# Row maxima moved from the seam into the projection's batches

## The reference

```python
q = jnp.einsum('oc,bct->bot', Wq, target) + bq[None, :, None]   # target = layernorm(x)
k = jnp.einsum('oc,bcs->bos', Wk, source) + bk[None, :, None]   # source = ctx_2048
v = jnp.einsum('oc,bcs->bos', Wv, source) + bv[None, :, None]
dot = jnp.einsum('bhdt,bhds->bhts', q, k) / math.sqrt(HEAD_DIM)
mask = target_mask[:, :, :, None] * source_mask[:, :, None, :]
dot = mask * dot - (1.0 - mask) * NEG                           # NEG = 1e6
amap = jax.nn.softmax(dot, axis=-1) * mask
out = jnp.einsum('bhts,bhds->bhdt', amap, v)
```

## Time and profile before

| | us |
|---|---|
| median of 3 runs | 1266.68 (1265.74 to 1266.74) |
| profiled execution | 1268.15 |
| its span | 1266.3 |
| PE, DVE busy in the span | 1089.0, 1033.0 |
| ACT, POOL busy in the span | 672.6, 515.0 |
| first score matmul | 170.10 |

### The profile page before, as it was taken

How to read it: one execution, slowest core, us unless ns; L and a number is a source line. 1 busy time by engine, 2 the same in 40 slices (tenths; PEclk the granted TensorE clock), 3 DMA queues, 4 the chain that set the end, 5 groups by cost and what they waited for, 6 DMA issues and landing times. The chain is left out here.

```text
span 1266.3 us, 14046 instructions
## 1 busy us (share of the span) xinstructions
PE 1089.0 (86%) x4802; PEld 424.1 (33%) x4802; DVE 1033.0 (82%) x1568; ACT 672.6 (53%) x787; POOL 515.0 (41%) x403
## 2 busy tenths in 40 slices
PE   4977689999999999778999976999999997189586
PEld 2543112222222222134444433444444443134232
DVE  5679779999999999378999964887888888776898
ACT  1655148888888888946566652110000000786896
POOL 2765221535435436520101014878888883000021
PEclk9989569999999999999999996999999999599889
DMA  9799852446446444132111101121211110000011
GB/s 325 246 306 334 258 181 93 131 129 200 119 141 195 129 146 121 49 122 109 34 51 49 35 20 46 56 64 53 67 54 62 61 55 17 1 1 1 9 59 66
DMA packets 74215, 132.89 MB, mean 105 GB/s; under 512 B 18848, under 2 KB 37664, under 8 KB 73632
## 3 DMA queue, kind: packets, MB, share of 16 engines
q1 hardware_dynamic: 74144, 132.00, 32.4%
HBM read 107.58 MB, written 22.02 MB: 102 GB/s over the span
## 5 line engine op out<-in xcount | busy, mean ns | idle before, releaser
L821 DVE TENSOR_REDUCE mneg<-ps_m 128x1 f32<-128x512 f32 x512 | 324.9, 683 | 38.2 <-PE ps_m L738 34.2
L1383 PE MATMUL ps_y<-kv,toeplitz_sb 128*128 128x512 f32 x640 | 280.4, 597 | 9.8 <-POOL kv L1295 9.8
L696 ACT ACTIVATE probs<-ps_s 128x1024 f32<-128x1024 f32 x256 | 250.7, 1023 | 39.7 <-PE ps_s L760 39.6
L1383 PEld LDWEIGHTS ps_y<-kv,toeplitz_sb 128*128 128x128 f32 x640 | 121.4, 192 | 156.7 <-issue 156.7
L760 PE MATMUL ps_s<-qk_stack 128*128 128x512 bf16 x512 | 138.9, 386 | 23.2 <-ACT probs L696 17.5
L738 PE MATMUL ps_m<-qk_stack 64*128 64x512 bf16 x512 | 126.0, 411 | 14.5 <-DMA qk_stack<-mask_k 12.5
L770 PE MATMUL ps_o<-probs,v_all 128*17 128x512 f32 x1024 | 135.6, 602 | 0.2 <-ACT probs L696 0.2
L1295 POOL TENSOR_TENSOR kv<-vT,ctxT_sb 128x2048 f32<-128x2048 f32 x32 | 118.7, 3710 | 41.2 <-PE ps_y L1383 33.4
L1001 PE MATMUL ps_g<-w,xT_f 128*128 128x512 bf16 x512 | 119.3, 382 | 11.4 <-DVE h_f L1167 7.9
L1449 DVE TENSOR_TENSOR z<-ps_y,ctxT_sb 128x1024 f32<-128x1024 f32 x64 | 77.9, 1217 | 48.1 <-PE ps_y L1383 48.1
L1348 ACT ACTIVATE w_anchor<-w_f 128x512 f32<-128x512 f32 x32 | 20.1, 628 | 180.6 <-DMA w_f<-in_w 180.6
(11 more groups left out here) (159 smaller groups left out, 1624.7 us busy)
## 6 DMA issues: line engine op xcount, KB each, us to landing
qk_stack<-qk_parts SPq DMA_DIRECT2D x192, 128.0 KB, 4.0
w_sweep<-in_w SPq DMA_DIRECT2D x8, 1536.0 KB, 10.9
qk_parts<-qk_part SPq DMA_DIRECT2D x48, 256.0 KB, 4.6
w_sweep<-in_w SPq DMA_DIRECT2D x16, 768.0 KB, 5.2
w_sweep<-in_w SPq DMA_DIRECT2D x16, 512.0 KB, 3.7
toeplitz_sb<-in_toeplitz SPq DMA_DIRECT2D x32, 256.0 KB, 2.6
w_f<-in_w SPq DMA_DIRECT2D x32, 256.0 KB, 2.9
v_rows<-vp SPq DMA_DIRECT2D x8, 544.0 KB, 10.3
```

The source lines that it names most:

```text
L696: nc.scalar.activation(pr[:, k % 2, 2 * slot:2 * slot + 2, :], S[:, 2 * slot:2 * slot + 2, :], ACT.Exp).then_inc(exp_done, 1)
L821: nc.vector.tensor_reduce(mneg[:, h, tc, hd:hd + 1], M[:, bank(j), :], AX.X, ALU.max, negate=True).then_inc(max_red, 1)
L1383: mm = nc.tensor.matmul(Y[:, q % 3, l2, :], T[:, g % 2, (lt - m) * P:(lt - m + 1) * P], kv[:, g % 2, m, :], start=(m == 0), stop=(m == lt))
```

## The change

1. **Maxima.** 38 of the 48 tiles of the seam are taken inside batches 3 to 7, in pairs (`ahead`), four pairs a batch at fixed places: behind the keys, behind the queries, in the middle of the values and behind them. Batch 7 has three. A pair uses banks 0 and 1 of `ps_m` and waits until the pair before is reduced. Unit 0 is then finished in batch 6, its maxima are turned in batch 7 and its row copied by ACT there. Ten tiles of unit 1 are left for `vector_first`, now behind the weight totals. `ps_a` of the projection takes all eight banks of PSUM, and `ps_m` lies over its banks 4 to 6; the values, which used banks 4 to 7, now share banks 6 and 7 (`VP`), so that the pairs have banks 4 and 5.
2. **Engines.** ACT normalises the rows (scale and a shift `xa_shift`) and masks the values. In batch 7 its three weight sums stand ahead of the first copy.
3. **Loads.** Unit (0,0) is loaded in batch 1, (0,1) in batch 3, (1,0) in batch 7 between the stores of keys and of queries, and (1,1) at the end. The mask rows and leading parts of a unit have one semaphore (`qk_lead`), the rest another (`qk_rest`). A store of parts is one DMA of 768 KB instead of three of 256 KB.
4. **Memory.** `qk_r` is gone, the rest is written over `qk_f`; the buffers are ordered so that those freed first lie under stack 2 and attention's own first loads.

```diff
 def load_unit(core, sp, b, h):
     slot = 2 * (b % 2) + h
+    sp.wait_ge(core.qk_stored[b % 2], 32 * (b // 2 + 1))
+    for a in range(2):
+        for dst, src in ((core.Q, core.mask_q), (core.K, core.mask_k)):
+            heads = dst[slot][:, QUAD * a:QUAD * (a + 1), :]
+            sp.dma_start(heads[SIDE * a + LEAD:SIDE * (a + 1):STEP],
+                         src[:, b].unsqueeze(1).to_broadcast([HD, QUAD, L])).then_inc(core.qk_lead[slot], 16)
...
-                         .rearrange("d s x l -> d s (x l)"), both[:, a]).then_inc(core.qk_loaded[slot], 16)
+                         .rearrange("d s x l -> d s (x l)"), both[:, a])\
+                .then_inc((core.qk_lead if blk < LEAD else core.qk_rest)[slot], 16)
...
         for b in range(B):
+            if b == B - 1:
+                load_first(sp)
             store_parts(b, KS)
             if b + RING < B:
                 load_ctx(b + RING)
+            if b == B - 1:
+                load_next(sp, 0)
             store_parts(b, QS)
...
-            if b == B - 3:
                 sp.wait_ge(rows_stored, 32)
-                sp.wait_ge(qk_stored[0], 96)
                 load_unit(core, sp, 0, 0)
-            if b == B - 1:
+            if b == 3:
                 load_unit(core, sp, 0, 1)
...
         for b in range(B):
+            if b == B - 1:
+                for m in range(3):
+                    sum_weights(b, m)
             part1(b, KS)
-            if b:
+            if 1 <= b < B - 1:
+                normalise(b + 1)
                 sum_weights(b, 0)
+            if b == B - 1:
+                rows_of_first_max(act)
             part2(b, KS)
             part1(b, QS)
-            if b:
+            if 1 <= b < B - 1:
                 sum_weights(b, 1)
             part2(b, QS)
+            mask_values(b)
...
         for b in range(B):
             keys(b)
+            ahead(pe, b, 0)
             if b == 0:
                 values(b)
             queries(b)
+            ahead(pe, b, 1)
             if b:
                 values(b)
+            ahead(pe, b, 3)
...
+    def ahead_pairs(b, part):
+        n = 4 * (b - FIRST) + part - (b == B - 1)
+        return range(max(n, 0), n + 1) if b >= FIRST and not (b == B - 1 and part == 0) else range(0)
+
+    def tensor_pair(pe, q):
+        v, h = q // (TILES // 2), q // (TILES // 2)
+        if q % (TILES // 2) == 0:
+            pe.wait_ge(qk_lead[h], LEADS)
+        if q == TILES // 2:
+            pe.wait_ge(mrow_ready, 1)
+        if q:
+            pe.wait_ge(max_red, 2 * q)
+        for a in range(2):
+            leading_products(pe, h, (2 * q + a) % TILES, a)
...
+def load_first(sp):
+    load_batch(sp, 0, 0)
+    place_max(sp, 0, 0, 0)
+def load_next(sp, h):
+    if h == 0:
+        sp.wait_ge(wsum_ready, 3 * B)
+        load_unit(core, sp, 1, 0)
+    else:
+        sp.wait_ge(k_done, B)
+        sp.wait_ge(v_done, B)
+        load_weights(sp, 0, 0)
+        sp.wait_ge(f_ready, 2 * B)
+        load_unit(core, sp, 1, 1)
+        load_weights(sp, 1, 1)
```

More of the change, by code:

```diff
@@ L197, in store_parts @@
             sp.wait_ge(p3_ready, nth(b, s))
-            for j in range(3):
-                sp.dma_start(core.parts[s, b, j].rearrange("(ct p) l -> p ct l", p=P), part[:, b % 2, s, j])\
-                    .then_inc(qk_stored[b % 2], 16)
+            sp.dma_start(core.parts[s, b].rearrange("j (ct p) l -> p (j ct) l", p=P),
+                         part[:, b % 2, s].rearrange("p j ct l -> p (j ct) l")).then_inc(qk_stored[b % 2], 16)
         def store_values(b):
@@ new lines, in place_max @@
+    def place_max(sp, v, slot, h):
+        sp.wait_ge(mrow_ready, v + 1)
+        for a in range(2):
+            row = SIDE * (1 - a) + MAX_ROW
+            sp.dma_start(Q[slot][row:row + STEP + 1:STEP, QUAD * a:QUAD * (a + 1), :], mrow[UH * a:UH * (a + 1)])\
+                .then_inc(m_placed[h], 16)
+    def load_first(sp):
[12 more added lines that the diff above has]
+            load_weights(sp, 1, 1)
@@ L663, in gpsimd, with rows_of_first_max @@
             batch(b, b % 2, b == 0, b == B - 1)
+    def rows_of_first_max(act):
+        act.wait_ge(m_turned, 1)
+        nc.scalar.activation(mrow[:], RT0[0:2 * UH, 0:L], ACT.Copy).then_inc(mrow_ready, 1)
     def scalar(act):
@@ L667, in rows_of_max @@
             act.wait_ge(m_turned, v + 1)
-            if not same(v, 0):
-                act.wait_ge(m_placed[1 - h], 32 * before)
+            act.wait_ge(m_placed[1 - h], 32 * before)
             nc.scalar.activation(mrow[:], RT[0:2 * UH, 0:L], ACT.Copy).then_inc(mrow_ready, 1)
-        rows_of_max(0, 0, 0)
-        act.wait_ge(rows_stored, 32)
         act.wait_ge(q_done, B)
         act.wait_ge(v_done, B)
-        act.wait_ge(p3_ready, 2 * B)
+        for p in range(2):
+            act.wait_ge(v_stored[p], 16 * (B // 2))
         def evacuate(u, h, G, bu):
@@ L716, in scalar, with tensor_ahead, leading_products @@
         over_batches(act, batch)
+    def ahead_pairs(b, part):
[9 more added lines that the diff above has]
+            pe.wait_ge(max_red, 2 * q)
+        for a in range(2):
+            leading_products(pe, h, (2 * q + a) % TILES, a)
+    def tensor_ahead(pe, b, part):
+        for q in ahead_pairs(b, part):
+            tensor_pair(pe, q)
+        if b == B - 1 and part == 0:
+            pe.wait_ge(m_split, 1)
+            for tc in range(LT):
+                mm = nc.tensor.transpose(RT0[0:2 * UH, tc * P:(tc + 1) * P], mm16[:, 0, tc, :], core.ident16[:])
+            mm.then_inc(m_turned, 1)
     def tensor_first(pe):
-        pe.wait_ge(qk_loaded[0], LOADS)
+        for q in range(AHEAD, 3 * TILES // 4):
+            tensor_pair(pe, q)
         pe.wait_ge(vt_ready, LT * B)
-        for tile in range(HALF):
-            max_tile(pe, 0, 0, tile, HALF + tile)
-        for tile in range(HALF, TILES):
-            max_tile(pe, 0, 0, tile, tile - HALF)
+        pe.wait_ge(o_cleared, 1)
+    def leading_products(pe, slot, tile, bank_):
+        a, hd, tc = place(tile)
+        rows = slice(SIDE * a, SIDE * (a + 1))
+        nc.tensor.matmul(M[:, bank_, :], Q[slot][rows, hd, tc * P:(tc + 1) * P], K[slot][rows, hd, :],
+                         start=True, stop=True).then_inc(max_mm, 1)
     def max_tile(pe, v, slot, tile, j):
-        a, hd, tc = place(tile)
         n = TILES * v + tile
@@ L732, in max_tile @@
             pe.wait_ge(mrow_ready, v)
-        elif TURN_SLOT <= j < TURN_SLOT + 2:
+        elif TURN_SLOT <= j < TURN_SLOT + 2 or (v == 1 and j < 2):
             pe.wait_ge(max_red, n - 1)
-        elif not (same(v, 0) and tile < 3):
+        else:
             pe.wait_ge(max_red, n - 2)
-        rows = slice(SIDE * a, SIDE * (a + 1))
-        nc.tensor.matmul(M[:, bank(j), :], Q[slot][rows, hd, tc * P:(tc + 1) * P], K[slot][rows, hd, :],
-                         start=True, stop=True).then_inc(max_mm, 1)
+        leading_products(pe, slot, tile, bank(j))
     def tensor(pe):
@@ L856, in vector @@
     def vector(dve):
-        for tile in range(HALF):
-            reduce_tile(dve, 1, 1, tile, HALF + tile)
         def batch(b, par, first, last):
```

259 lines of the change are left out of this document (132 added, 127 removed).

## The result

| | before | after |
|---|---|---|
| median, 11 runs each on one chip, us | 1266.43 (1264.89 to 1267.32) | 1269.11 (1267.96 to 1272.01) |
| ratio to before | | 1.0023 [1.0015, 1.0032] |
| profiled execution, span | 1268.15, 1266.3 | 1270.36, 1268.6 |
| T, weights of batch 7 used | 125.4 | 144.4 (forecast 141.3) |
| first exponential | 172.53 | 175.98 (forecast 171.5) |

The change makes the kernel 2.7 us slower. The forecast was 1265.6, so it is 3.5 us off. Of the 3.45 us by which the first exponential is late, 2.9 are still there at the end of attention.

The account below looks back on a forecast made before the run. The projection was taken as bound by DMA through the masks batches wait for, and the first exponential as deciding the end. T +16.0 (9.5 + 5.2 + 1.3) and a tail 17.0 shorter gave -1.0: 1265.6 us, range 1257 to 1273.

Parts of the forecast that it names:

- The step that failed: how much of two unit loads is new ahead of T: Projection: the early loads of units (0,0) and (0,1) put 3.2 MB more ahead of T, 9.5 us later at 334 GB/s.
- A path called hidden: Batch 3: PE waits for unit 0's leading parts until 80.7 us, queries and values behind; hidden, since mask 4 lands at 92.
- 5.2: From 71.3 to 84 us SP issues only unit (0,0) into an empty queue; 1.7 MB are missing, 5.2 us.
- 1.3: Batches 0 and 1: ACT's longer chain with POOL costs 3 us, fewer store issues return 1.7; net +1.3, bounds 0 and +4.
- The tail: From T to the first exponential: 47.2 us before, T+30.2 after, so 17.0 us shorter.
- Chain (b): PE's chain from T: pairs of maxima and batch 7's values, first score at T+28.9, exponential at T+31.3 or T+29.6.
- a mixture: PE's clock in batch 7, between half and full: full for the second half of values gives T+29.6, half gives T+31.3.
- (a): SP's chain from T: stores and unit (1,0), values issued at T+24.4, landed T+28.8, first exponential T+30.2; taken to decide.
- B: Rival: the engines catch up the queue time lost from 71 to 84 us; T only 9.5 later, 1259 us; chance 0.27.
- C: Rival: the loop of mask, queries, POOL, store and later mask sets the pace, batches 5 to 7 4.8 later; 1270.5; chance 0.10.
- D: Rival: unit loads cost their issue time even in a full queue, 7.6 us more than the forecast, 1273 us; chance 0.08.
- A: The forecast itself: the queue takes back what the seam gives; 1265.6 us, own range 1262 to 1269.5; chance 0.55.

Follow-up runs that it names:

- e2: Changed kernel with unit (0,1) loaded in batch 5 instead of batch 3, behind the weights of batch 7; 1264.97 us, ratio 0.9980.
- e11: Kernel before with the load of unit (0,0) also made a second time, in batch 3; ratio 1.0067.
- e12: Changed kernel with a unit's 12 transfers of parts issued ahead of the wait for the mask tables and of its mask rows; ratio 1.0010.
- e10: Changed kernel with unit (0,0) loaded in batch 2 instead of 1, mask tables still stored in batch 1; 1274.74 us, ratio 1.0065.
- e3: Changed kernel with the projection's 38 reductions reading 8 of 512 columns, so their maxima are not the true ones; 1271.28 us, ratio 1.0033.
- e9: Kernel before with the two mask tables stored in batch 0 instead of batch 1; ratio 0.9995.
- e6: Changed kernel with tables stored in batch 0, unit (0,1) loaded in batch 5, and batch 7's values and weights ahead of unit (1,0); 1257.3 us, ratio 0.9928.
- e1: Changed kernel with batch 7's queries' parts and values stored, then unit 0's weights loaded, ahead of unit (1,0); 1266.19 us, ratio 0.9995.
- e5: Kernel before with the engine edit alone: ScalarE normalises the rows and masks the values; ratio 1.0017.
- e8: e7 with batch 3's four pairs taken in the middle of its values and behind them, two at a time; 1250.50 us, ratio 0.9874.
- e7: e6 with unit (1,1) loaded behind the placing of row 1 of unit 1's maxima instead of ahead; 1252.08 us, ratio 0.9894.

## Why the prediction was wrong

The mechanism held in the main: the first exponential decides, and it is late by what SP's queue holds. Of the signs that I had named, the maxima of batch 3 (not before 80) came at 81.04, the values' store ended the table load, and DMA was near full behind 84 us (0.95). The sizes were off: mask 4 at 96.9 (near 92), mask 7 at 143.3 (near 137), T at 144.4 (near 141), DMA at 0.44 from 71 to 84 (0.6). PE's wait for the row of maxima in batch 7 was to be 5 us and more, and the whole gap there is 1.97. The miss at the first exponential, 175.98 against 171.5 (taken from the forecast of T+30.2), is 4.5 us in two terms.

1. **The step that failed: how much of two unit loads is new ahead of T.** I wrote "of the 2.0 left I put half before T, 1.0 MB" and so let 3.2 MB stand ahead of it, 9.5 us. But the load of unit (0,0) began at 116.10, behind the weights issued at 114.01, so in the kernel before it was hardly ahead of T, and moving it took little off. e2 put the second load behind those weights and T came 7.8 us earlier, and e11 put one more load ahead of them and T came 6.3 later. Two loads are 12.6 us, not 9.5, and the 3.1 missing are as large as the 3.1 by which T came late, 144.4 instead of 141.3. The bytes agree: up to T the engines moved 125.3 us x 303 GB/s = 38.0 MB before and 144.4 x 289 = 41.7 MB after, 3.8 MB more where I had 3.2. At the 303 of before that is 12.4 us, and the lower rate is the other 6.7. No run took the load of unit (0,0) alone out of batch 5, and the first of its parts, issued at 116.10, had landed 7.7 us later, ahead of T; so some of the 1.0 MB was rightly taken off, and the term is known to 1 or 2 us.
2. **A path called hidden.** I wrote that PE's wait for the leading parts, with queries and values of batch 3 behind it, "is hidden, since mask 4" lands at 92. The wait ended as forecast, 81.04 (80.7), but the work behind it took until 96.55: it would have held batch 4 there with any mask. In e12 the mask was 4.4 us earlier and batch 4 was not. e10 is the same path made longer: PE at 91.25, mask 4 at 105.95. That T was late by this path is not shown, as e12's T came 3.4 us earlier with batch 4 where it was.
3. **The rest of T**, 19.0 - 12.6 = 6.4, was forecast as 5.2 + 1.3 = 6.5. The tables went out 1.7 us later than before (61.35 against 59.67), which answers to the 1.3, but with the same code they went out at 59.98 in e3 and e12, so this fit is partly luck. For the other 5.2 the sum is right and the reason half so: e9 shows 5.3 us for the tables' 8 us of issuing alone, which the kernel before already paid, and e12 gives 2 to 3.4 for the wait. That such costs add up is an assumption; it held in e12, but in e6 3 to 5 us of 15.8 were missing.
4. **The tail**, 31.6 instead of 30.2: the values were issued at T+24.6 (forecast T+24.4), but landed 5.7 us later and not 4.4, since unit (1,0), the parts and the weights were in flight beside them; 4.4 was read from an emptier moment. Chain (b) was to be at T+28.9 with its score and was at T+24.3. The queries of batch 7 ran eight matmuls in 3.70 us, full clock, and the stretch from 140 to 160 us had 0.91; I had taken a mixture, and my sign of a long wait for the row failed with it. It didn't matter here, since (a) decided, but it is why e1 gained 6.0.
5. **Prices of engines.** Masked values take 0.42 us each (1.69 for four), forecast 0.55; rows 0.75, forecast 0.81. By e5 and e3 neither the moved work nor the reductions set T in the changed kernel; once the transfers are in time (e6 to e8), the engines' pace does. The 0.17% that e5's medians lost is near the 0.23% of the whole change, and its place is open.
6. **Rivals.** B fell: T moved by 19.0, not 9.5. C fell: at batch 6 VectorE waited 7.0 us for the mask and not for the chain. D fell by e11. I had given faster 0.41 and slower 0.24. The two terms together, 3.1 + 1.3, carry A from the middle of no change over its upper border.

The Trainium skill (DMA: Bandwidth & Descriptors, section Bandwidth) has 138 GB/s for 64 KB, measured on transfers that GpSimd issued; by this figure 20 transfers of 64 to 128 KB would cost 15 us or so of a queue, as an estimate. e11, with SP issuing, measured 6.3. As I read it the page gives a transfer's own time; for many in flight this case's run disagrees, and the measurement decides. The Trainium skill (TensorE: Matmul & The Clock Gate, section A second HAM failure mode: psum-queue depth-cycling) has a kernel whose groups cycle through PSUM banks with small idles between them and whose clock keeps switching. In batch 7 that was so for a small part: the granted clock was 0.91 from 140 to 160 us with pairs between the groups, and in e7 it was 1.00 from 84 to 120 us.
